# Last attention: which operand of the probability-value product stands still in TensorE, and VectorE's share of the low halves

## The reference

```python
xf = x.reshape(t, d)
probs = jax.nn.softmax(xf @ Wg.T + bg, axis=-1)
...
qkv = xf @ Wqkv.T + bqkv + delta
...
attn = jax.nn.softmax(jnp.einsum('bhsd,bhtd->bhst', q, k) * SCALE, axis=-1)
out = jnp.einsum('bhst,bhtd->bhsd', attn, v)
out = jnp.transpose(out, (0, 2, 1, 3)).reshape(b, s, d)
return out @ Wproj.T + bproj
```

## Time and profile before

| | |
|---|---|
| median of three runs | 2971.27 us |
| the profiled execution's own time | 2969.1 us |
| its span | 2967.3 us |
| TensorE busy (matmul) | 2651.6 us, 89% |
| weight loads, beside the matmuls | 1938.8 us, 65% |
| VectorE busy | 1584.1 us, 53% |
| ScalarE busy | 777.7 us, 26% |
| GpSimd busy | 1277.2 us, 43% |
| the six pairs of the last attention | 2205.3 to 2883.5 us of the span |

### The profile page before, as it was taken

The page is one execution under the profiler, slowest core; times in us unless marked ns, Lnnn a source line. Parts: engine busy times, 40 slices in busy tenths (PEclk is TensorE's granted clock), DMA queues, the critical chain, the costliest instruction groups (busy, mean ns, idle before and its releaser), DMA issues.

```text
span 2967.3 us, 65252 instructions
## 1 busy us (share of the span) xinstructions
PE 2651.6 (89%) x22950; PEld 1938.8 (65%) x22950; DVE 1584.1 (53%) x2845; ACT 777.7 (26%) x1100; POOL 1277.2 (43%) x1363
## 2 busy tenths in 40 slices
PE   5998999978998769999999898876769999999999
PEld 4787888847676557888885667754545556555555
DVE  7566666664545553333334354544775745746731
ACT  2111121201222212111220132211134355354350
POOL 1684211147777710000006677774415274274372
PEclk9999999999999979999999899987979999999999
DMA  5233333459989932333237988997310000000013
GB/s 165 90 127 103 121 123 118 146 197 314 321 298 307 313 126 90 104 121 99 94 99 251 331 291 302 323 339 241 96 38 1 22 22 1 22 22 1 22 48 94
DMA packets 102525, 440.92 MB, mean 149 GB/s; under 512 B 19881, under 2 KB 20204, under 8 KB 98081
## 3 DMA queue, kind: packets, MB, share of 16 engines
q0 software_dynamic: 55712, 266.88, 26.4%
q1 hardware_dynamic: 44001, 131.65, 13.8%
q10 hardware_dynamic: 2592, 39.32, 3.7%
HBM read 357.66 MB, written 80.08 MB: 148 GB/s over the span
## 4 chain that ended last, share of the span: by engine, by line
PE 59%; DVE 16%; issue 7%; POOL 7%; DVEq 4%; DMA 4%; ACT 2%; POOLq 0%; SPq 0%; ACTq 0%
PE PS L1709 26%; PE PS L2057 6%; PE PS L1719 3%; PE PS L1987 3%; PE PS L1808 3%; POOL GATA L685 2%; PE PS L1902 2%; DVE NMC L1630 2%; PE PS L2044 2%; PE PS L1846 2%; POOL ROW L685 2%; PE PS L2045 2%; POOL PL L736 2%; PE PS L1840 2%; PE PS L1860 1%
## 5 line engine op out<-in xcount | busy, mean ns | idle before, releaser
L1709 PE MATMUL PS<-WHL,XT 128*125 (+1 forms) x2880 | 487.2, 329 | 7.1 <-DVE WHL L1092 4.2
L1709 PE MATMUL PS<-WHL,HT 128*125 (+1 forms) x2880 | 477.1, 329 | 12.0 <-DVE HT L1245 9.4
L1709 PEld LDWEIGHTS PS<-WHL,HT 128*125 (+1 forms) x2880 | 395.3, 138 | 90.1 <-DVE HT L1245 10.6
L1709 PEld LDWEIGHTS PS<-WHL,XT 128*125 (+1 forms) x2880 | 390.8, 137 | 82.9 <-issue 4.7
L736 POOL TENSOR_TENSOR PL<-PF 125x500 bf16<-125x500 f32 (+1 forms) x360 | 322.4, 928 | 216.4 <-ACT PF L949 215.5
L685 POOL DMA_INDIRECT GATA<-msg_table,SKEY x324 | 311.1, 960 | 138.2 <-issue 96.1
L1179 DVE SCALAR_TENSOR_TENSOR MSG<-PS,MSG 125x768 f16<-125x768 f32 x160 | 153.0, 956 | 360.8 <-ACT MSG L775 358.9
L775 ACT ACTIVATE MSG<-PS 125x768 f16<-125x768 f32 x160 | 129.6, 810 | 794.7 <-PE PS L1709 794.7
L2057 PE MATMUL PS<-PF,V 125*128 125x500 bf16 (+1 forms) x720 | 244.6, 352 | 16.0 <-POOL PL L736 14.4
L685 POOL DMA_INDIRECT ROW<-msg_table,SKEY x216 | 213.0, 986 | 83.6 <-issue 59.6
L949 ACT ACTIVATE PF<-PS,QK 125x500 f32<-125x500 f32 (+1 forms) x360 | 213.5, 608 | 124.3 <-PE PS L2045 118.1
(11 more groups left out here) (316 smaller groups left out, 4803.4 us busy)
## 6 DMA issues: line engine op xcount, KB each, us to landing
msg_table<-MSG SPq DMA_DIRECT2D x160, 336.0 KB
WST<-in_wg_dram ACTq DMA_DIRECT2D x16, 2304.0 KB, 9.9
WST<-in_wf_dram SPq DMA_DIRECT2D x7, 1536.0 KB, 6.8
KROW<-key_rows POOLq DMA_DIRECT2D x54, 192.0 KB, 3.8
WST<-in_wm_dram SPq DMA_DIRECT2D x6, 1152.0 KB, 5.5
msg_table<-MSG SPq DMA_DIRECT2D x160, 39.0 KB
GATA<-msg_table,SKEY POOLq DMA_INDIRECT x324
ROW<-msg_table,SKEY POOLq DMA_INDIRECT x216
```

Of the source, the lines that this page charges most:

```text
L1709: ins = pe.matmul(PS[0:ROWS, b0 + h, 0:HALF], X[:, xp, k, bass.ts(t, ROWS)], panel_part(slot, wp, k, h), start=k == 0 and xp + wp == 0, st ...
```

## The change

Three things, all in the last attention.

1. The probabilities become the weights, 125 queries at a time (a block), and the values move. One row of `V2` is now 64 low features, 64 high features and a one (129 columns). The high half of the probabilities meets all 129, the low half the last 65. The result is query by feature in 125 partitions; a chunk has four blocks (two of 250), three in one bank and the fourth in the next, so that O takes two banks: 4 and 5, or 6 and 7 in turn. The scores keep banks 0 to 3.
2. `normalise` adds the two halves, multiplies by the reciprocal of the sum, and writes `HR`, query by feature. TensorE transposes `HR` in three pieces X0 to X2 of the next pair's start, behind q0 (behind the last pair for the last one), and ScalarE copies them into `HF`.
3. Every third low half (k % 3 == 2) is made by VectorE, in `low_part`, ahead of the normalisation that follows.

```diff
+        for c in range(3):
+            FFN.append((f"X{c}", "act", ((0, 1, 0)[c],)))
...
-                FFN.append((f"O{h}{c}", "dve", (6 + (3 * h + c) % 2,)))
+                FFN.append((f"O{h}{c}", "dve", ((4, 5), (6, 7))[(3 * h + c) % 2]))
...
-            FFN.append((f"S{h}{c}{t}", "act", (n_ % 6,)))
+            FFN.append((f"S{h}{c}{t}", "act", (n_ % 4,)))
...
+                    if n_ % 3 == 2:
+                        continue
                     g.wait_ge(S["ffn_act"], ffn.taken(it, f"S{h}{c}{t}"))
...
+                def output_columns(c, to):
+                    c0, n = CHUNKS[c]
+                    act.wait_ge(S["ffn_pe"], ffn.made(it, f"X{c}"))
+                    act.activation(HF[:, bass.ds(to, 1), c0:c0 + n].rearrange("p a c -> p (a c)"), PS[:, ffn.bank(f"X{c}"), 0:n], ACT.Copy).then_inc(S["ffn_act"], 1)
+
                 for r in HIGHS:
+                    if r == "k0":
+                        for c in range(3):
+                            output_columns(c, (it + PAIRS - 1) % PAIRS)
...
-                r, o = RCPF[:, 0, 0:n], HF[64 * h:64 * h + 64, bass.ds(it, 1), c0:c0 + n].rearrange("p a c -> p (a c)")
-                v.reciprocal(r, psum[64:128, 0:n])
-                v.drain()
-                return v.tensor_tensor(o, psum[0:64, 0:n], r, ALU.mult)
+            def normalise(b, n, c0, h):
+
+                for b_, q0, nq in ((b, 0, min(3, n // ROWS)), (b + 1, 3, n // ROWS - 3)):
+                    if nq > 0:
+                        sums = PS[0:ROWS, b_, 0:nq * 129].rearrange("p (q d) -> p q d", d=129)
+                        t0 = c0 // ROWS + q0
+                        v.reciprocal(DEN[:, 0:nq], sums[:, :, 128])
+                        v.tensor_copy(HN[:, 0:nq, :], sums[:, :, VLO])
+                        v.drain()
+                        v.tensor_tensor(HN[:, 0:nq, :], sums[:, :, VHI], HN[:, 0:nq, :], ALU.add)
+                        v.drain()
+                        ins = v.tensor_tensor(HR[:, t0:t0 + nq, 64 * h:64 * h + 64], HN[:, 0:nq, :], DEN[:, 0:nq].unsqueeze(2).broadcast_to([ROWS, nq, 64]), ALU.mult)
+                        v.drain()
+                return ins
...
+                def low_part(n_):
+                    h, c, t = n_ // 30, n_ // 10 % 3, n_ % 10
+                    n = CHUNKS[c][1]
+                    v.wait_ge(S["ffn_act"], ffn.taken(it, f"S{h}{c}{t}"))
+                    v.tensor_tensor(PL[:, n_ % PARTED, 0:n], PF[:, n_ % PARTED, 0:n], PH[:, n_ % PARTED, 0:n, 1], ALU.subtract).then_inc(S["ffn_lo2"], 1)
...
+                    h = int(r[1])
+                    if r[0] == "O":
+                        for n_ in range(2, 2 * 3 * RT, 3):
+                            k = 10 * (3 * h + int(r[2])) + 9 + LAG
+                            if k - 10 < n_ <= k or (r == "O00" and n_ <= k) or (r == "O12" and n_ > k):
+                                low_part(n_)
...
+            def output_transposes(c):
+
+                c0, n = CHUNKS[c]
+                for k in range(n // ROWS):
+                    ins = pe.transpose(PS[:, ffn.bank(f"X{c}"), k * ROWS:(k + 1) * ROWS], HR[:, c0 // ROWS + k, :], IDF[0:ROWS, 0:ROWS])
+                ins.then_inc(S["ffn_pe"], 1)
...
-                        o = PS[:, ffn.bank(f"O{h}{c}"), 0:n]
-                        parts = (PH[:, k % PARTED, 0:n, 1], PL[:, k % PARTED, 0:n])
-                        for vp, pp in ((0, 0), (0, 1), (1, 0)):
-                            ins = pe.matmul(o, V2[:, vp, t, h, :], parts[pp], start=t == 0 and vp + pp == 0, stop=t == RT - 1 and vp == 1)
+                        b = ffn.bank(f"O{h}{c}")
+                        for q in range(n // ROWS):
+                            o, rows = PS[0:ROWS, b + q // 3, q % 3 * 129:q % 3 * 129 + 129], slice(q * ROWS, (q + 1) * ROWS)
+                            pe.matmul(o, PH[:, k % PARTED, rows, 1], V2[:, t, h, 0:129], start=t == 0 and q % 3 == 0, stop=False)
+                            ins = pe.matmul(o[:, VSUM], PL[:, k % PARTED, rows], V2[:, t, h, VSUM], start=False, stop=t == RT - 1 and q in (2, n // ROWS - 1))
```

More of the change, by code:

```diff
@@ L224, in graph_and_attentions_kernel @@
         LMAX, LPOW, LALL, QKS, QKINV, SINV, SSCALE = (slice(n_, n_ + 1) for n_ in range(7))
-        V2 = sb(fctx, "V2", [ROWS, 2, RT, 2, 128], bf16)
+        V2 = sb(fctx, "V2", [ROWS, RT, 2, 130], bf16)
+        VLO, VHI, VONE, VSUM = slice(0, 64), slice(64, 128), slice(128, 129), slice(64, 129)
+        HR = sb(fctx, "HR", [ROWS, RT, 128], f32)
+        DEN = sb(fctx, "DEN", [ROWS, 4], f32)
+        HN = sb(fctx, "HN", [ROWS, 3, 64], f32)
         NM = sb(fctx, "NM", [ROWS, 2 * RT], f32)
@@ L234, in graph_and_attentions_kernel @@
         IDB = sb(fctx, "IDB", [128, 128], bf16)
-        RCPF = sb(fctx, "RCPF", [64, 1, 500], f32)
         fctx.close()
@@ L721, in _ @@
             g.drain()
-            g.memset(V2[:, 0, :, :, 64:128], 1.0)
-            g.drain()
-            g.memset(V2[:, 1, :, :, 64:128], 0.0)
+            g.memset(V2[:, :, :, VONE], 1.0)
+            g.memset(HR[:], 0.0)
             g.drain()
@@ L949, in _ @@
                     act.activation(PF[:, n_ % PARTED, 0:n], p, ACT.Exp, scale=QK[0:ROWS, SSCALE]).then_inc(S["ffn_act"], 1)
+            for c, (c0, n) in enumerate(CHUNKS):
+                act.wait_ge(S["ffn_pe"], ffn.made(PAIRS, f"X{c}") - ffn.made(0, "X0") + 1)
+                act.activation(HF[:, PAIRS - 1, c0:c0 + n], PS[:, ffn.bank(f"X{c}"), 0:n], ACT.Copy).then_inc(S["ffn_act"], 1)
         @block.vector
@@ L1609, in v_low @@
                     v.wait_ge(S["ffn_hi"], it * 9 + (HIGHS.index(f"v{c}") + 1))
-                    low, high = (V2[:, p_, t0:t1, :, 0:64].rearrange("p t h d -> p (t h) d") for p_ in (1, 0))
+                    low, high = (V2[:, t0:t1, :, p_].rearrange("p t h d -> p (t h) d") for p_ in (VLO, VHI))
                     v.scalar_tensor_tensor(low, PS[0:ROWS, ffn.bank(f"v{c}"), 0:(t1 - t0) * 128].rearrange("p (n d) -> p n d", d=DH),
                                            SC[0:ROWS, XWINV], high, ALU.mult, ALU.subtract).then_inc(S["ffn_dve"], 1)
+                def low_part(n_):
[3 more added lines that the diff above has]
+                    v.tensor_tensor(PL[:, n_ % PARTED, 0:n], PF[:, n_ % PARTED, 0:n], PH[:, n_ % PARTED, 0:n, 1], ALU.subtract).then_inc(S["ffn_lo2"], 1)
                 for r in LOWS:
@@ L1632, in _ @@
                         c0, n = CHUNKS[int(r[2])]
-                        normalise(PS[:, ffn.bank(r), :], n, c0, it, h).then_inc(S["ffn_dve"], 1)
+                        normalise(ffn.bank(r), n, c0, h)
+                        v.sem_inc(S["ffn_dve"], 1)
                         v.drain()
@@ L1996, in _ @@
                     if r[0] in "qkvO":
+                        continue
+                    if r[0] == "X":
+                        ffn.wait_banks(pe, it, r)
+                        if it:
+                            pe.wait_ge(S["ffn_dve"], ffn.taken(it - 1, "O12"))
+                        else:
+                            pe.wait_ge(S["ffn_ready"], 1)
+                        output_transposes(int(r[1]))
                         continue
@@ L2062, in _ @@
                             ins.then_inc(S["av_done"], 1)
+            pe.wait_ge(S["ffn_dve"], ffn.taken(PAIRS - 1, "O12"))
+            for c in range(3):
+                ffn.wait_banks(pe, PAIRS, f"X{c}")
+                output_transposes(c)
             pe.wait_ge(S["wp_in"], 32)
-            pe.wait_ge(S["ffn_dve"], ffn.taken(PAIRS - 1, "O12"))
+            pe.wait_ge(S["ffn_act"], ffn.taken(PAIRS, "X2"))
             for i in range(RT // 2):
```

11 lines of the change are left out of this document (6 added, 5 removed).

## The result

The changed kernel takes 3018.72 us (median of four runs, 3017.14 to 3031.45), the kernel before on the same chip 2969.45 us (2967.39 to 2975.25): a ratio of 1.0172 [1.0140, 1.0204]. Forecast were 2988 us, within 2955 to 3008. So the direction was right, the size was not, and the time lies outside the range.

The account below looks back on a forecast made before the run. TensorE's work, or what it waits for, was taken to set a pair's length; +0.6 us a pair (+3.6 for six), clock +12.6 and tail +1.6, together +18 on 2969.1, gave 2988 us, range 2955 to 3008.

Parts of the forecast that it names:

- Products: Last attention's products on TensorE: 200 blocks a pair at 0.115 us make 23.0 instead of 32.6, -9.6 us a pair.
- The three waits: TensorE's idle times: behind the split +3.6 us a pair, ahead of q0 +1.2, at X2's transposes +3.9.
- the tail: Behind the last pair: the 2.44 us wait becomes normalising, transposes and two waits on ScalarE, +1.6 us.
- The lock between VectorE and GpSimd: Low halves: one engine runs while the other stands; waits where a normalisation holds VectorE's low half, +1.5 us a pair.
- The clock: Six pairs: twelve drops to 1.2 GHz at 1.5 us make 18, less 5.4 already there, +12.6 us in all.
- The other terms: Products and waits without the clock: +0.6 us a pair, +3.6 for six pairs.
- The clock holds at X2: Rival: the 2.8 us idle at X2 brings no drop, six drops go, 2979 us; chance 0.2.
- Loads cost nothing beyond the columns: Rival in the product step: 0.081 us a block, VectorE and GpSimd then pace, 2964 us; chance 0.16.
- loads pace at 0.116 each: Rival in the product step: products take 46.4 us a pair, +120, 3108 us; chance 0.03.
- The split stall doesn't grow: Rival behind the split: VectorE is through before TensorE has used its lead, about 2962 us; chance 0.06.
- the case of dear loads: Rival in the product step: weight loads set the pace; 3108 us, or 3082 by the skill's 104 ns; chance 0.03.
- drops of two lengths: Clock drops behind the split twice as long, one of two reasons given for the range's upper end, 3008 us.

Follow-up runs that it names:

- run 3: The changed kernel with the third piece of transposes, X2, in bank 2 instead of X0's bank 0: 3003.03 us, 1.0093 of the kernel before.
- run 5: The changed kernel with O's two bank pairs exchanged, so that q0's bank 6 is free: 3009.86 us, 1.0104 of the kernel before.
- run 6: The changed kernel with VectorE's split of the next weights cut into five pieces between its low halves: 2986.57 us, 1.0025 of the kernel before.
- run 1: The kernel before with every third low half on VectorE, values still the weights: 3026.06 us, 1.0150 of the kernel before.
- run 2: The changed kernel with all low halves on GpSimd again: 3015.80 us, 1.0128 of the kernel before.
- run 4: The changed kernel with the first score matmul of steps 49 to 54 issued two or four times more: 3019.99 us, 1.0145 of the kernel before.
- run 11: The changed kernel with weight loads of 128 probability columns instead of 125, no wait repaired: 2995.62 us, 1.0070 of the kernel before.
- run 10: The changed kernel with X2 in bank 2, O's banks exchanged, split in pieces, all low halves on GpSimd: 2985.39 us, 1.0011 of the kernel before.

## Why the prediction was right and wrong

**Products: right.** 0.115 us a block, from the 58 ns of the earlier trace rows, is what the trace shows, and its loads do pass 0.06 us apart; with 128 columns it is 0.088, not far from the lower bound of 0.081 that the earlier trace rows, also with 128-column weights, had given. The rule of the Trainium skill weighed there (the page "TensorE: Matmul & The Clock Gate", LDWEIGHTS) would have had 0.208; the trace disagrees.

**The three waits: right,** each within half a microsecond. 5.2 to 5.4 us behind the split (5.7 forecast; low half 44 took 0.7 of the 1.4 counted for it), 1.21 ahead of q0 (1.5), 2.57 ahead of X2 (2.8). Runs 3, 5 and 6 take them away one by one, and each makes the kernel faster. That the tail came within 0.1 us is luck in part: its terms add up to +1.4 and not to the +1.6 written there, the normalising was shorter than forecast (1.21 for 1.5 us), and from there to the output product it took 2.96 us at half clock, where 0.9 + 1.4 were counted.

**The lock between VectorE and GpSimd: as forecast in kind.** VectorE's 500 low half lasts 1.54 us where 0.53 is its own work. Small waits for low halves, of 0.44 to 1.09 us, add up to 1.7 us in the second pair and 2.8 in the third, beside 0.5 before; the forecast had +1.5 for them, as waits behind the normalisations. The 0.95 us for a low half of GpSimd in that sum stands in no row: alone, four of 500 pass in 3.96 us.

**The clock: this step failed.** "Twelve drops at 1.5 us": their number was nearly right (eleven), their length was not. I took the 3.3 us of the kernel before, whose products behind the wait are 500 columns wide, for a length that any drop has. Behind the split it was 6.8 us twice and 23.9 us four times. Runs 1 and 2 show that the products and not the wait make the difference, run 4 that no long drop stays with wide matmuls among the blocks, run 11 that none stays with 128-column loads. By the busy time at half clock the clock cost some 42 us, where 12.6 were forecast: 30 too few. The other terms together came to about nothing, where +3.6 was forecast, as the waits were a little shorter; so the pairs missed their sum by 26.3 us. The lengths say the same: from its first score to its last product the stage takes 61.3 to 62.2 us with a long drop and 58.0 or 58.1 with a 6.8 us one, and the next pair up to its first score about 2 us more. The 5.5 us of the earlier stages are no part of the change, as far as the trace shows; they are about the spread of the runs of before.

**The rivals.** "The clock holds at X2" fell: it dropped there in five of six pairs. "Loads cost nothing beyond the columns" and "loads pace at 0.116 each" both fell with the 0.115 block. "The split stall doesn't grow" fell with the 5.2 us. The 3082 us given with the case of dear loads, summed as the 3108 beside it (18.6 less 3.4 us a pair), would be 3079. None of them had a longer drop in it, and the range's upper end allowed for it with words only ("drops of two lengths"), at 20 us above the forecast, where 31 came.

**Open.** Why two of six drops behind the split last 6.8 us and four 23.9, with the same instructions in each, no run tells; in runs 3 and 5, with the same blocks, two and three of six were 6.8 us too. So blocks behind 125-column loads can bring the clock back, and mostly did not. Nor do the runs tell which property of the 125-column load matters to the clock, its duration or something else of it, or what lets the clock fall in run 10.
